# Moving the third batch's routing and the first group's placement into steps 15 and 16, and the first tiles of the last feed-forward between the last attention values

## The reference

```python
hn = _layernorm(x, ln1_g, ln1_b)
q, k, v = ...                       # hn @ wq + bq and so on, 16 heads of 8
attn = jax.nn.softmax(q k^T / sqrt(8))
x = x + (attn v @ wo + bo)
hn2 = _layernorm(x, ln2_g, ln2_b).reshape(-1, h)
idx = jnp.argmax(hn2 @ gate_w + gate_b, axis=-1)
mid = jax.nn.relu(hn2 w1[e] + b1[e])    # 128 -> 512, e = idx of the token
y = mid w2[e] + b2[e]                   # 512 -> 128
return x + y
```

## Time and profile before

| | us |
|---|---|
| median of three runs | 1168.8 |
| lowest, highest | 1159.86, 1170.2 |
| the profiled execution, its own time | 1171.29 |
| its span in the profile | 1169.5 |

### The profile page before, as it was taken

How to read it: one execution, slowest core, us unless ns; L and a number is a source line. 1 busy time by engine, 2 the same in 40 slices (tenths; PEclk the granted TensorE clock), 3 DMA queues, 4 the chain that set the end, 5 groups by cost and what they waited for, 6 DMA issues and landing times.

```text
span 1169.5 us, 15387 instructions
## 1 busy us (share of the span) xinstructions
PE 929.6 (79%) x5738; PEld 499.9 (43%) x5738; DVE 610.4 (52%) x1637; ACT 437.2 (37%) x750; POOL 216.5 (19%) x214
## 2 busy tenths in 40 slices
PE   4777886997757786396599788877889889887898
PEld 2333453663423343274266333333334334342676
DVE  5444564445453534233743443447687777672554
ACT  2233423342422322011232323233776776664333
POOL 1100051533241112102521100001010000004254
PEclk9789887998976757599789878896999999997999
DMA  9600001231334000012100100000000000003020
GB/s 292 241 1 1 1 28 45 89 88 43 118 92 148 8 7 22 23 46 56 24 1 9 36 1 1 1 1 0 2 1 2 1 1 2 1 1 127 24 87 10
DMA packets 41056, 49.23 MB, mean 42 GB/s; under 512 B 5801, under 2 KB 30658, under 8 KB 40344
## 3 DMA queue, kind: packets, MB, share of 16 engines
q1 hardware_dynamic: 36184, 39.20, 10.9%
q0 software_dynamic: 4800, 9.05, 2.6%
HBM read 33.52 MB, written 19.82 MB: 46 GB/s over the span
## 4 chain that ended last, share of the span: by engine, by line
PE 58%; DVE 22%; issue 7%; POOL 5%; ACT 4%; DMA 3%; SPq 1%; POOLq 0%; DVEq 0%; ACTq 0%
PE PS L180 50%; DVE KB L2024 4%; DVE KB L1624 4%; PE PS L653 3%; POOL RB L2318 1%; POOL OT L2233 1%; DVE Ht L1528 1%; DVE st L1515 1%; POOL d L2308 1%; DVE OT L1667 1%; PE PS L1128 1%; ACT PT L1278 1%; POOL ve L2216 1%; ACT KB L1422 1%; DVE CX L1667 1%
## 5 line engine op out<-in xcount | busy, mean ns | idle before, releaser
L2024 DVE TENSOR_REDUCE KB<-PS 128x2 fp32r<-128x1024 f32 x128 | 154.5, 1221 | 46.8 <-PE PS L180 45.5
L1278 ACT ACTIVATE PT<-PS 77x512 f32<-77x512 f32 x192 | 98.0, 590 | 183.3 <-PE PS L180 183.3
L180 PE MATMUL PS<-CX 32*77 32x512 f32 (+2 forms) x896 | 129.3, 596 | 18.2 <-DVE OT L1667 7.3
L2216 POOL TENSOR_TENSOR ve<-ve,nh 128x4 f32<-128x4 f32 x40 | 41.5, 1039 | 473.9 <-DVE ve L1523 473.9
L1624 DVE TENSOR_REDUCE KB<-PS 128x16 fp32r<-128x1232 f32 x48 | 69.1, 1439 | 71.6 <-PE PS L180 71.6
L180 PE MATMUL PS<-RA,RB 128*128 x152 | 85.1, 643 | 9.1 <-issue 4.5
L1442 ACT ACTIVATE PT<-PS 128x1024 f32<-128x1024 f32 x74 | 75.6, 1023 | 38.2 <-PE PS L180 37.0
L180 PE MATMUL PS<-QB,KB 64*128 64x512 f32 x256 | 60.6, 471 | 19.3 <-DVE KB L2024 14.9
L180 PEld LDWEIGHTS PS<-CX 32*128 32x128 f32 (+1 forms) x896 | 48.0, 196 | 65.1 <-issue 21.7
L180 PE MATMUL PS<-PT,VB 77*32 77x512 f32 x384 | 61.3, 716 | 17.6 <-DVE KB L1624 13.4
L180 PE MATMUL PS<-KB,QB 64*128 64x512 f32 x256 | 66.0, 516 | 4.8 <-DVE KB L2024 3.2
(11 more groups left out here) (302 smaller groups left out, 1621.8 us busy)
## 6 DMA issues: line engine op xcount, KB each, us to landing
RB<-d SPq DMA_DIRECT2D x10, 256.0 KB, 3.0
o<-CX SPq DMA_DIRECT2D x10, 256.0 KB, 2.4
RA<-in_l_w SPq DMA_DIRECT2D x1, 2304.0 KB, 10.4
d<-OT SPq DMA_DIRECT2D x2, 1024.0 KB, 6.8
RB<-in_l_w SPq DMA_DIRECT2D x1, 2048.0 KB
RA<-in_l_w SPq DMA_DIRECT2D x1, 2048.0 KB, 15.4
RB<-d SPq DMA_DIRECT2D x3, 514.0 KB, 3.9
CX<-d SPq DMA_DIRECT2D x3, 514.0 KB, 4.9
```

Of the source, the lines that this page charges most:

```text
L180: return e.matmul(o, l, r, start=first, stop=last, skip_group_check=True)
L1278: e.activation(slot[s][0:NK, :], PS[0:NK, 4 + j, :], ACT.Exp, bias=0.0, scale=a.scale).then_inc(*expd(i, r, j))
L2024: e.tensor_reduce(o, PS[:, k:k + 2, :], AX, ALU.max).then_inc(*rmax("s", s, t, p2))
L2216: e.tensor_tensor(ve[:, 8 * par + 4:8 * par + 8], ve[:, 8 * par:8 * par + 4], nh[:, :], ALU.pow).then_inc(*rstd(*key))
```

## The change

It does four things. The pieces of `route3(2)` get earlier times in step 15 (and `tail4(2)` in step 14 slightly later ones), two further pieces of it move from step 16 into step 15, and the last three come at 0.02 to 0.12 of step 16 instead of 0.14 to 0.68. `place3(0)` is spread over step 16 from 0.15 on, at 33 pieces per step, where it came from 0.7 on at 25. The loop ends one step earlier, and what was step 18 (the last products of `third(15)` and the values of `fourth(15)`) is written out; the first five pieces of `experts3` (`turn3(0)`, `up(0)`, `up(1)`, `turn3(1)`, `middle(0)`) stand between the last values. For that the buffers of the hidden layer move from the slots to `Ht`, `HT` and a part of `CX`, which are free since the last queries and keys were made, and the first tiles take single banks of 0 to 6.

```diff
@@ -297,6 +297,8 @@
+        hid3 = [Ht[:, 0:512], Ht[:, 512:1024], HT[:, 0:512]]
+        hidT3 = [HT[:, 512:1024], CX[:, 3072:3584], CX[:, 3584:4096]]
...
-                        m = e.transpose(PS[:, k, 128 * c:128 * c + 128], slot[i % 3][:, 128 * c:128 * c + 128], ident[:, :])
+                        m = e.transpose(PS[:, k, 128 * c:128 * c + 128], hid3[i % 3][:, 128 * c:128 * c + 128], ident[:, :])
...
-                        m = mm(e, PS[:, k, 0:128], slot[3 + i % 3][:, 128 * c:128 * c + 128],
+                        m = mm(e, PS[:, k, 0:128], hidT3[i % 3][:, 128 * c:128 * c + 128],
...
                     banks.only(range(7), True)
-                elif name == "experts3":
-                    banks.only(range(8))
...
         def p3_free(step, i):
 
-            return e3.at(step, i - 3) if i >= 3 else weighed.at("s", 15, 3)
+            return e3.at(step, i - 3) if i >= 3 else projected.at("s", 15) if step == "d" else projected.at("n", 3, 1)
...
-            for i in range(19):
+            for i in range(18):
...
                 if i == 14:
                     end = tail4(2)
-                    streams.append((islice(end, 5), [0.56, 0.64, 0.72, 0.8, 0.92]))
+                    streams.append((islice(end, 5), [0.66, 0.74, 0.82, 0.9, 0.97]))
...
                     streams.append((norms, [0.14]))
                 if i in (8, 12, 15):
                     routing = route3((i - 7) // 4)
-                    streams.append((islice(routing, 14), [0.22, 0.33, 0.37, 0.47, 0.7, 0.71, 0.81, 0.82, 0.84, 0.87, 0.9, 0.93, 0.96, 0.99]))
-                if i in (9, 13, 16):
+                    streams.append((islice(routing, 14), [0.22, 0.31, 0.35, 0.43, 0.63, 0.64, 0.72, 0.74, 0.76, 0.78, 0.81, 0.83, 0.86, 0.89] if i == 15 else [0.22, 0.33, 0.37, 0.47, 0.7, 0.71, 0.81, 0.82, 0.84, 0.87, 0.9, 0.93, 0.96, 0.99]))
+                if i == 15:
+                    streams.append((islice(routing, 2), [0.95, 0.99]))
+                if i in (9, 13):
                     streams.append((routing, [0.14, 0.2, 0.24, 0.65, 0.68]))
                 if i == 16:
-                    streams.append((place3(0), 25, 0.7))
+                    streams.append((routing, [0.02, 0.08, 0.12]))
+                    streams.append((place3(0), 33, 0.15))
                 weave(*streams)
-            hook("experts3")
+            weave((scores[17], [0.02, 0.145, 0.27]), (islice(values[17], 2), [0.05, 0.175]))
+            hook("banks", range(7))
+            tiles = experts3()
+            weave((values[17], [0.3, 0.425, 0.485, 0.505]), (islice(tiles, 5), [0.32, 0.4, 0.43, 0.46, 0.5]))
+            hook("banks", range(8))
 
             def last_route():
                 yield from tail4(3)
@@ -2695,7 +2702,7 @@
 
             route_at = [0.2, 0.8, 1.4, 2.0, 4.6, 6.0, 8.0, 9.2, 10.0, 11.4, 13.2, 14.0, 15.2, 17.2, 17.6, 17.9, 18.2, 18.5, 18.8, 19.2, 20.2, 21.0, 21.8,
                         22.6, 23.4, 24.2, 24.6, 25.1, 25.6, 26.2, 26.7, 27.0, 27.3, 27.8, 28.1, 29.0, 30.0, 31.0, 32.0, 33.0]
-            weave((experts3(), 1), (last_route(), route_at))
+            weave((tiles, 1), (last_route(), route_at))
```

More of the change, by code:

```diff
@@ L1485, in up @@
                         w.wait_ge(*p3_free("m", i))
-                        e.activation(slot[i % 3], PS[:, banks.of(a3e, "u", i), :], ACT.Copy).then_inc(*a3e("u", i))
+                        e.activation(hid3[i % 3], PS[:, banks.of(a3e, "u", i), :], ACT.Copy).then_inc(*a3e("u", i))
                     yield
@@ L1496, in middle @@
                         for c in range(4):
-                            m = e.activation(slot[3 + i % 3][:, 128 * c:128 * c + 128], PS[:, k, 128 * c:128 * c + 128], ACT.Relu,
+                            m = e.activation(hidT3[i % 3][:, 128 * c:128 * c + 128], PS[:, k, 128 * c:128 * c + 128], ACT.Relu,
                                              bias=BS[g][:, 4 * n + c:4 * n + c + 1], scale=1.0)
@@ L2139, in up @@
                         w.wait_ge(*p3_free("m", i))
-                        e.tensor_copy(slot[i % 3], PS[:, banks.of(d3e, "u", i), :]).then_inc(*d3e("u", i))
+                        e.tensor_copy(hid3[i % 3], PS[:, banks.of(d3e, "u", i), :]).then_inc(*d3e("u", i))
                     yield
@@ L2150, in middle @@
                         for c in range(4):
-                            m = e.tensor_scalar(slot[3 + i % 3][:, 128 * c:128 * c + 128], PS[:, k, 128 * c:128 * c + 128],
+                            m = e.tensor_scalar(hidT3[i % 3][:, 128 * c:128 * c + 128], PS[:, k, 128 * c:128 * c + 128],
                                                 BS[g][:, 4 * n + c:4 * n + c + 1], 0.0, ALU.add, ALU.max)
```

## The result

The changed kernel takes **1173.0 us** (median of 20 runs, 1170.9 to 1182.5), the kernel before 1168.7 in runs beside it: ratio **1.0051, 95% interval 1.0032 to 1.0070**. That is 4.4 us slower where I forecast 1 us faster; within 1%, and inside the range of 1158 to 1174, but on the other side of the old time. The profiled execution has a span of 1172.8 us, 3.3 more than before.

A forecast was written before the change was run, and what follows sets the result against it. PE was taken as the main bound (58% of the span), with DVE also nearly full in step 16. Paid 5.2 less won 6.2 gave -1.0 us: 1170.3 profiled, 1168 us as median; range 1158 to 1174.

The forecast's parts named there:

- (a): First tile: PE's standstill waiting for the read of the sorted rows goes, winning 4.0 us.
- (b): Behind that wait: 5.4 us of PE work at clock 0.51 run at full clock, winning 2.7 us.
- (c): At route3(3): PE's 1.79 us wait for DVE's normalised rows grows, costing 0.5 us.
- rival B: Step 16: PE takes most of the delay in; delay 1.8 us or none, time 1164.4 down to 1159; chance 0.28.
- What is paid: step 16: Steps 15 and 16: moved DVE work makes the last maxima's transposes, L1000, 5.2 us later.
- The transposes of VX now stand where PE waited 0.86 us, which hides them (0.55 us): Step 15: the last product starts 0.55 us earlier, at 1035.2.
- Ranks too early for DVE: End of step 15: PE waits 2.0 us at rt,tri for DVE's running sum.
- The bank 6 chain: Start of step 16: L1000 waits for ACT's L1467; b2 ends at 1044.0, without the bank 1042.3.
- DVE as the bound: Step 16: seven maxima (8.05 us) and place work (6.7 us) in series; last maximum ends at 1059.55.
- rival C: Step 16: clock falls after the wait at the ranks, 3 us lost; 1171 us, up to 1174; chance 0.17.
- D: First tile: rows come late because busy DVE holds up eight writes; read 9.6 us later, 1172 us; chance 0.05.
- The other sign: From the last tile's start to the kernel's end: time doesn't move; otherwise the forecast fails as a whole.

The follow-up runs named there:

- place_early: Kernel before plus the tiles between the last values and the change's early places, routing as before; ratio 0.9953.
- T_only: tiles_only with only the transposes of VX (L1044) moved earlier in step 15, as in the change; ratio 1.0029.
- tiles_only: Kernel before plus only the tiles between the last values; routing and places at their old times; ratio 1.0002.
- place_late: The change with the places of group 0 back at their old time, routing early as in the change; ratio 1.0056.
- filled pairs: Batch 3's ranks and choice transposes moved early, without and with two extra PE products before the wait: on tiles_only 1.0053, 1.0030; on place_early 1.0024, 0.9999.
- T_back: The change with the transposes of VX (L1044) back at their old time; ratio 1.0044.
- moves_only: The change without the tiles between the last values; routing and places moved; ratio 1.0026.
- place_spread: Kernel before plus the tiles between the last values and the places of group 0 spread lightly by an explicit list; routing as before; ratio 0.9978.
- spread2: place_spread with later tail4(2), the first two batches' places a little earlier, and only the tiles' first transposes between the values; ratio 0.9916.
- ranks_fill: tiles_only with batch 3's ranks and choice transposes moved to the end of step 15, plus two extra PE products ahead of the wait; ratio 1.0030.
- spread3: spread2 with the first group's place items at earlier points of step 16; ratio 0.9885, 1156.6 us.

## Why the prediction was wrong

**Gains: right in sum, and partly by luck.** 6.2 us were forecast, and M to the end is 5.7 shorter (-6.0 and +0.3; the first tile now stands ahead of the last values, so only the sum of the two is to be compared). The 4.02 us for `RB<-d` of the earlier trace rows are gone. The rows came early enough, though later than forecast: the first write starts 31.4 us behind A2 (1052.39; I had 26.3), the last at 1067.57. Not all of (a) and (b) came as put: `up(0)` waits 1.61 us for ACT's scaled tiles (L1479), a term I took as even with another, and a part of the tile's first stretch is still slow (0.79 where it was 0.51). (c) was right: the wait of 1.79 us at `route3(3)` became two, 1.22 and 1.01 us, that is 0.4 more where I had 0.5. What I left out is that early rows can win more: in place_early, where the clock is 0.99 from M to the tile (0.79 in the change), M to the end takes 104.7 us, 10.5 less than before. I had put a gain of that kind into rival B only. In the change the slow clock takes most of it back, and so the sum looks right.

**The step that failed is "What is paid: step 16"**: 5.2 us forecast, 11.8 measured. Up to the first product of step 16 I had 16.4 us from A2 (1040.2 - 1023.8); it was 19.3 (1040.33 - 1021.00), 2.9 more. From there to M I had 19.35; it was 23.04, 3.7 more. By its parts:

- *"The transposes of VX now stand where PE waited 0.86 us, which hides them (0.55 us)"*: wrong. I asked when PE would be free and not when the bank would be. The transposes take bank 6, which ACT had not yet read. The wait alone is 1.56 us where I had a gain of 0.55, and in T_only's profile the move costs 3.3 us up to M.
- *Ranks too early for DVE*: the mechanism was right, and in the kernel with only this move the wait is as forecast (2.07, forecast 2.0). In the change it is 0.65, because PE came there late, at half clock. The bank 6 chain L1467, L1000, L1432, b2 stands in the trace as walked, with waits of 0.58 and 0.36.
- *DVE as the bound*: wrong for most of the step. I added seven maxima and 6.7 us of place work in series. place_early has the place work between the maxima too and is only 3.0 us longer to M than tiles_only. In the change PE waits for a maximum for over a microsecond only twice in step 16 (1.02 and 2.08 us, around L2119); ahead of these two, up to 1052, it is PE at half clock that takes the time.
- *The clock*: I held it at 1.00 in the forecast and gave its fall to rival C with 3 us. 8.6 of the 11.8 us are PE's longer instructions, by the account above.

That the time still lies within the range is luck in part: a DVE bound that mostly wasn't there stood in for a clock that fell.

**The rivals.** C was right in kind and sign (1171 forecast, 1173.0 measured) and too small: I priced only what PE does between one maximum and the next product, and let the fall begin at `rt,tri`, while it began some 7 us earlier, between L1044 and the gates, lasted to 1052, and came back at 1060. B (PE takes the delay in) is out. D (late rows) is out too: PE waited for no DMA at the tile. Its working rested on the first write's 1.08 us as the price of a busy DVE, but the earlier trace rows left out the second one: in the kernel before it took 1.14 us, begun just ahead of L2119 (last section), and in the change the first write takes 1.08 us again while the two behind it, beside the same busy DVE, take 0.99.

The other sign that I had named, the time from the last tile's start to the end, did not move: 20.4 us before, 20.3 after.

**What is shown, and what not.** That the routing's move costs: place_late against tiles_only, whose intervals don't touch, and the change against place_early. That the places' move wins: place_early lies 0.5% under tiles_only; these two intervals overlap by 0.0005, but the difference, 0.0049, is larger than the error of the two together (0.0039). That a wait at `rt,tri` of some 2 us brings the half clock, and that the half clock is a price of its own, beside the wait: by the filled pairs, 1.0 and 2.4 us in the slow stretch that follows, and in the whole time only by the two pairs taken together. That the 1.56 us at L1044 alone set off the 20 us at half clock is not shown: T_back lost that wait and kept the slow stretch, T_only had it and was back at full clock 4.3 us later, and place_late had it and kept the full clock up to `rt,tri`. moves_only, with the change's order, shows the change's slow stretch again. In the change, where this wait and those of the ranks, bank 6 and L2119 follow each other, I can't say which of them keeps the clock down.

## What to carry to other kernels

When PE's work is moved to an earlier place, look up for each moved instruction three times: when PE is there, when its operands are, and when the other reader of its PSUM bank is done; a gap in PE's timeline is no free place if the bank is still held. A new wait of PE costs more than its length where the clock falls behind it: here 1.0 and 2.4 us more for waits of 2.07 and 2.08 us, by the filled pairs. Since not every such wait brings the fall, treat it as a risk and look at the granted clock in the trace. When two moves are made together, run each by itself: here one was worth 0.5% and the other cost 0.5 to 1%.

## What the runs showed of the hardware

**Short waits in a nearly full stretch can bring the half clock, and not every time.** PE was busy for 4.91 and 3.44 us of the two 5 us windows ahead of the fall in the change, with one wait of 1.56 us; the clock then was at 0.50 for some 20 us, though PE was busy for 4.0 to 5.0 us of each 5. The same wait at L1044 gave a clock of 0.83 for 10 us in T_only and 1.00 in place_late, up to its next wait. Behind a wait of 1.06 us the clock fell in place_spread, behind 1.08 it didn't in spread2. tiles_only fell to 0.68 for 5 us though its waits in step 16 are those of the kernel before (0.85 us), which stayed at 1.00. And behind waits of 2.01 and 2.50 us for SP's rows the clock stayed full in ranks_fill and place_early. So the length of the wait doesn't settle it. The Trainium skill, TensorE: Matmul & The Clock Gate, "A second HAM failure mode: psum-queue depth-cycling", tells of this kind of loss: small idle spells between groups of matmuls, where PSUM banks are passed round, make the clock go down and up again. The traces agree in that the clock falls and returns in stretches with waits of 0.9 to 2.1 us; in the change a bank handed over 1.56 us late stands ahead of it, and the low clock is one long stretch of some 20 us.

**One DVE operation holds up one write from POOL.** The writes of the sorted rows take 0.97 to 0.99 us each (the first 1.08), but one took 1.94; beside it ran the widest DVE operation that reads two operands from SBUF, L2119:

```profile
1055.08 0.99 POOL L2283 DMA_INDIRECT d<-VB,ints  x1 [0.30 <-issue]
1056.37 1.94 POOL L2283 DMA_INDIRECT d<-VB,ints  x1 [0.30 <-DVE S L2117]
1058.61 0.98 POOL L2283 DMA_INDIRECT d<-VB,ints  x1 [0.30 <-issue]
```

```profile
1056.23 1.21 DVE L2119 TENSOR_TENSOR b1x<-S,b1t 128x608 f32<-128x608 f32 x1
```

The write started 0.14 us after L2119 and ended 0.96 us later than its neighbours would. It is the same in place_early (1.96 us beside an L2119 of 1.23, begun 0.13 before the write) and less in spread3 (1.57 us, where an L2119 of 1.26 had run for 0.54 already). In all three the write loses about what was left of L2119 when it started, less 0.1: 0.96, 0.99 and 0.60 us lost of 1.07, 1.10 and 0.72 left. The Trainium skill, SBUF — State Buffer, "SBUF: two separate sides", says that DVE and GpSimd share a pair of ports that goes to the first comer for its whole instruction, among others to a DVE operation with two SBUF operands when the GpSimd operation reads SBUF too. These three traces agree. The other order stands in the kernel before, and there nobody waited for the other's end: the write begun 0.31 us ahead of L2119 took 1.14 us, and L2119 its usual 1.19.

```profile
1056.91 1.14 POOL L2283 DMA_INDIRECT d<-VB,ints  x1 [0.31 <-DVE S L2113]
```

In the change it costs 1 us in twelve writes that PE doesn't wait for; the eight writes of rival D were too many by seven.
